# First experts' blocks: the next rows' halves ahead of the hidden units' low half, and a looser wait for the up product

## The reference, cut to what matters

```python
gates = softmax(xf @ router_w)
top_v, top_i = top_k(gates, 2)                       # two of 14 experts for each token
def _ffn(xn, rw, W1, W2):
    h = xn * rsqrt(mean(xn * xn) + RMS_EPS) * rw
    return silu(h @ W1) @ W2                         # 256 -> 512 -> 256
routed_out = sum over the two chosen experts of gate * _ffn(...)
shared = sum over 2 shared experts of _ffn(...)
x = x + tanh(g_ffn[0]) * (routed_out + shared)
```

## Time and profile before

| | |
|---|---|
| median of 3 runs | 928.59 us (927.75 to 929.23) |
| profiled execution: its time, its span from first to last instruction | 926.31 us, 924.6 us |
| busy over the span: PE, DVE, POOL, ACT | 723.6 (78%), 607.1 (66%), 484.5 (52%), 476.0 (51%) us |
| stretch of the 41 blocks: first and last start of L1541 | 412.5 and 567.0 us |

### The profile page before, as it was taken

How to read it: one execution, slowest core, us unless ns; L and a number is a source line. 1 busy time by engine, 2 the same in 40 slices (tenths; PEclk the granted TensorE clock), 3 DMA queues, 4 the chain that set the end, 5 groups by cost and what they waited for, 6 DMA issues and landing times. The chain is left out here.

```text
span 924.6 us, 21111 instructions
## 1 busy us (share of the span) xinstructions
PE 723.6 (78%) x6870; PEld 545.3 (59%) x6903; DVE 607.1 (66%) x1448; ACT 476.0 (51%) x969; POOL 484.5 (52%) x608
## 2 busy tenths in 40 slices
PE   3778999999884998978888888568876548998730
PEld 2445666666663898966666666457766426665520
DVE  6665777777766699834444443687878346667766
ACT  3545666666563677723333332336654246776632
POOL 5796788798301468830000001785955716756455
PEclk9998999999998699989999999698989779999975
DMA  7344444433201468742222221478521213323233
GB/s 168 90 104 121 111 116 119 104 105 82 56 3 23 163 205 260 233 129 64 69 69 69 67 67 47 133 209 206 161 81 54 75 45 108 112 81 99 81 91 103
DMA packets 87664, 98.96 MB, mean 107 GB/s; under 512 B 17260, under 2 KB 77132, under 8 KB 87564
## 3 DMA queue, kind: packets, MB, share of 16 engines
q1 hardware_dynamic: 63468, 66.10, 24.4%
q0 software_dynamic: 16432, 24.66, 10.0%
q10 hardware_dynamic: 7664, 6.89, 2.6%
HBM read 61.03 MB, written 24.38 MB: 92 GB/s over the span
## 5 line engine op out<-in xcount | busy, mean ns | idle before, releaser
L783 DVE TENSOR_REDUCE a_mx<-ps 112x2 f32<-112x750 f32 x128 | 120.2, 939 | 52.1 <-PE ps L401 50.5
L673 POOL DMA_DIRECT2D a_stkK<-a_KS x248 | 118.7, 487 | 21.1 <-issue 15.4
L643 ACT ACTIVATE a_Pf<-ps 125x672 f32<-125x672 f32 x128 | 90.0, 728 | 15.3 <-PE ps L345 14.1
L1830 POOL MEMSET a_half<- 112x2 f32 x1 | 0.1, 93 | 169.8 <-POOLq L89 169.8
L1541 DVE CAST f_hh<-ps 128x512 bf16<-128x512 f32 x41 | 28.4, 693 | 83.9 <-PE ps L1281 83.9
L51 PE MATMUL ps<-f_w2hi,f_hh 128*128 (+1 forms) x292 | 80.4, 275 | 3.7 <-DVE f_hl L1543 3.7
L51 PE MATMUL ps<-f_w2lo,f_hh 128*128 (+1 forms) x292 | 80.2, 275 | 0.0
L51 PE MATMUL ps<-f_w2hi,f_hl 128*128 (+1 forms) x292 | 80.2, 275 | 0.0
L2460 POOL TENSOR_TENSOR f_rl<-f_rf,f_rh 128x512 bf16<-128x512 f32 x34 | 39.4, 1160 | 63.6 <-DVE f_rh L2528 63.5
L1208 POOL DMA_INDIRECT f_xd<-xn,pos x32 | 56.8, 1774 | 22.9 <-issue 22.9
L1388 ACT ACTIVATE f_z<-ps 128x512 f32<-128x512 f32 x41 | 24.5, 597 | 85.1 <-PE ps L1281 85.1
(11 more groups left out here) (397 smaller groups left out, 2314.9 us busy)
## 6 DMA issues: line engine op xcount, KB each, us to landing
a_raw<-F_w SPq DMA_DIRECT2D x22, 512.0 KB, 5.2
f_xg<-f_xd SPq DMA_DIRECT2D x75, 128.0 KB, 2.3
f_yd<-f_yo SPq DMA_DIRECT2D x75, 128.0 KB, 1.7
f_raw<-F_w SPq DMA_DIRECT2D x14, 512.0 KB
a_ctxF<-ctxT SPq DMA_DIRECT2D x16, 375.0 KB, 3.2
a_cR<-ctx SPq DMA_DIRECT2D x16, 375.0 KB
a_stkK<-a_KS POOLq DMA_DIRECT2D x248, 23.4 KB, 2.0
a_cT_first<-ctxT SPq DMA_DIRECT2D x14, 375.0 KB, 4.0
```

What stands on the lines that cost most here:

```text
L643: nc.scalar.activation(Pf[:, j % PB], psST[:C, j % 2, :, 0:SC * T], ACT.Exp, scale=DH ** -0.5).then_inc(exp_done, 1)
L673: pool.dma_start(stkK[SIDE * h + DH * a:SIDE * h + DH * (a + 1), w.slot, jj], KS[2 * DH * jj + DH * h:2 * DH * jj + DH * (h + 1), w.odd, p ...
L783: nc.vector.reduce_max(mx[:, n.odd, j // JJ, :, j % JJ], maxima_of(n, j)[:T, :, :S], AX).then_inc(mx_red, 1)
```

## The change

Four edits, all in `l0_experts`:

- PE, `up_rows`: for blocks from the third on, the wait for `h_lo` (both halves of the hidden units two units back are made) is replaced by one for `act_done` (the silu two units back has read the bank). The wait for `t_lo` stays.
- PE: the register read for a block is issued a step earlier, right behind the up product of the block before, instead of right ahead of its own up product.
- ACT: in a step x_high(s + 3) comes ahead of silu(s + 2).
- DVE: `halves` is split in `half_high` and `half_low`; for blocks x_low(s + 3) comes between them.

```diff
                     pe.wait_ge(t_lo, s.block + 1)
-                    at_least(pe, h_lo, s.u - 1)
+                    if s.block < 2:
+                        at_least(pe, h_lo, s.u - 1)
+                    else:
+                        pe.wait_ge(act_done, s.u - 1)
...
-                        expert[n.u] = pe.value_load(bexp[0:1, n.block:n.block + 1], min_val=0, max_val=E0)
+                            expert[n.u] = expert_of(n)
                         up_rows(n, expert[n.u])
+                        if n.u + 1 < UNITS:
+                            expert[n.u + 1] = expert_of(units[n.u + 1])
...
+                    if t is not None:
+                        x_high(t)
                     if n is not None:
                         silu(n)
-                    if t is not None:
-                        x_high(t)
...
-                    if m is not None:
-                        halves(m)
+                    if m is not None and m.shared is None:
+                        half_high(m)
+                    if m is not None and m.shared is not None:
+                        half_low(m)
                     if t is not None:
                         x_low(t)
+                    if m is not None and m.shared is None:
+                        half_low(m)
```

More of the change, by code:

```diff
@@ L1311, in down, with expert_of @@
                     last.then_inc(y_full, 1)
+                def expert_of(s):
+                    return pe.value_load(bexp[0:1, s.block:s.block + 1], min_val=0, max_val=E0)
                 expert = {}
@@ L1535, in x_low, with half_high, half_low @@
                        ALU.subtract).then_inc(t_lo, 1)
-                def halves(s):
+                def half_high(s):
                     at_least(dve, y_full, s.u - 1)
-                    if s.shared is None:
-                        dve.wait_ge(z_full, s.block + 1)
-                        nc.vector.tensor_copy(like_hidden(s, hh), turned_hidden(s)).then_inc(h_hi, 1)
+                    dve.wait_ge(z_full, s.block + 1)
+                    nc.vector.tensor_copy(like_hidden(s, hh), turned_hidden(s)).then_inc(h_hi, 1)
+                def half_low(s):
+                    at_least(dve, y_full, s.u - 1)
                     dve.wait_ge(h_hi, s.u + 1)
```

## The result

The changed kernel takes 903.78 us at the median of 4 runs (901.91 to 906.68), the kernel before 928.91 in the same comparison. The ratio is 0.973 with a 95% interval of 0.969 to 0.977: faster. The profiled execution has a span of 900.2 us, against 924.6.

What follows compares the result with a forecast made beforehand. The prediction took the loop through PE and DVE, 3.90 us a step, as the bound, then PE's 3.27. 38 steps by 0.63 us are 23.9 us, taking the median 928.6 to 904.7; it forecast 904.5 us, range 901 to 911.

Steps and rivals of the forecast that it cites:

- The loop through DVE sets the old step: Blocks, old step of 3.90 us: 1.90 on PE, 1.75 on DVE, handing over 0.11 and 0.14; down product outside.
- The new loop is 3.17 us and PE's work 3.27: Blocks, changed step: next rows ready at 3.17 us, PE's gapless work 3.27, so PE bounds with 0.10 to spare.
- DVE's order, ACT's order and the wait are needed together: Blocks: ACT's old order would hold DVE until about 2.9 us; the old `h_lo` wait would leave nothing won.
- The register read costs nothing: PE, ahead of the transposes of `z`: 0.47 us read hidden by queued 1.30 us up product; taken as nothing.
- 38 steps by 0.63 us are 23.9 us: Blocks: 0.63 us gained in each of 38 steps, from 3.90 to 3.27, together 23.9 us.
- What is late next: Blocks: hidden units' low half ends about 3.8 us, needed at 5.23; silu ends at 3.2, transposes at 4.57; both covered.
- rival E: PE: register read waits for the products ahead; transposes start at 2.21, step 4.08 us, 935 us in all; chance 0.02.
- the limit of 2.04: PE: start of the transposes of `z`, in us after the up product's start, beyond which the change would be slower.
- The gain passes whole: Stage behind the blocks: starts from all engines' meeting point, so the full 23.9 us shortens the whole time.
- Rival C: Stages behind the blocks: some microseconds more at 1.2 GHz give gain back, 908 to 912 us; chance 0.06.

## Why the prediction was right

904.5 us was forecast, 903.78 measured. That they agree to 0.7 us is partly luck, since the four runs spread over 4.8 us; the step of 3.27 us forecast and 3.26 measured is what tests the mechanism. Point by point:

- *The loop through DVE sets the old step.* Shown from two sides. Taking 0.44 us from the down product leaves the old step at 3.90 us, and undoing any of the three other edits (DVE's order, ACT's order, the wait) lengthens the new step, to 3.98, 3.48 and 3.88.
- *The new loop is 3.17 us and PE's work 3.27.* Measured 3.17 with the shorter down product, and 3.26 in the changed kernel. The margin is 0.09 us by these two, 0.10 by the timeline.
- *DVE's order, ACT's order and the wait are needed together.* Without the first the step is 3.98, without the looser wait 3.88, without ACT's order 3.48, where 2.91 + 0.41 + 0.14 had given 3.46. So without either of the first two next to nothing of the gain is left, and without ACT's order a third of the 0.64 us is missing.
- *The register read costs nothing.* Right in the changed kernel, and the cover was rightly named: with two reads 0.43 us show. What the prediction did not see is that the move is not needed. In the old place the read runs while PE's sequencer waits for the rows' low half, and it is better covered there: two reads cost 0.01 us a step there, and 0.43 in the new place. With DVE's old order four long reads showed in the new place as well. So this edit is no part of the gain and gives away some cover.
- *38 steps by 0.63 us are 23.9 us.* Measured 24.3 on the stretch of the blocks.
- *What is late next.* The moved pieces stay covered, as forecast. The low half of the hidden units was put at "about 3.8" after the up product's start and ends at 3.62 (474.73 and 0.68, from 471.79); the silu was put at 2.6 and starts at 2.43. Neither was near the bound. In rival E the limit of 2.04 should be 2.03 (3.90 less 0.60, 0.11, 0.61, 0.41 and 0.14), which changes nothing.
- *The gain passes whole.* The whole time moved by 25.1 us between the medians and the profiled span by 24.4; the kernel with the read in its old place, with the same step, gained 21.9 in its own comparison. So the gain passes whole within about 3 us, and no closer than that. Rival C, a gain given back by the clock behind the stage, can't be told from scatter by one profile. There the last stretch took 5.1 us more at a mean granted clock of 0.84 instead of 0.86, but the kernel with two reads in the old place, whose blocks end within 4 us of the same point, has 356.7 us and 0.87 there:

```profile
541.20:897.90 356.70, 243.02 (x1686) 185.52 (x1685) 239.31 (x694) 181.64 (x448) 216.93 (x209) 0.87 0.38 108
```

So a shift of this size does not always bring a loss. Nor does the mean clock tell the length of this stretch: the changed kernel with 8 down matmuls has the same 0.84 there, and the shortest time of all twelve.

```profile
542.30:898.60 356.30, 247.93 (x1678) 191.05 (x1678) 238.15 (x695) 181.88 (x448) 216.50 (x209) 0.84 0.38 108
```

What makes this stretch 356 us long in one execution and 363 in another stays open.

## What to carry to other kernels

Write down the loop that closes through the wait that ends last, with every handing over in it, and beside it each engine's own work in a step. In four kernels here (before and changed, each with 12 and with 8 down matmuls) the step was the larger of the two, and both can be read from one step of the timeline. In a hand-ordered pipeline move ahead, on every engine of the loop, the piece that the next step waits for, and loosen the waits that would tie it to the pieces moved behind it: leaving out one of these edits cost nearly the whole gain or a third of it here. Then undo each edit of a change by itself: one of the four here was no part of the gain. For a change in one stage of a long kernel count the steps of that stage, since the rest can scatter by more than what is asked.

## What was not expected of the hardware

With the function split so that its second half waits for two semaphores instead of one, and with ACT's new order and the looser wait beside it, the distance between two dependent DVE instructions went from 0.73 to 0.79 us, and the typical step from 3.90 to 3.97 where this distance was on the loop; that the split is the cause is likely and not shown. And a register read on PE is free up to an edge: one between up product and transposes shows with nothing in the changed kernel, a second with 0.43 us. Where PE had waited before the up product, the edge was nearer: a read whose load took 0.30 us stayed hidden, and loads of 0.40 to 0.44 us showed with 0.05 to 0.09.
